# One-hots of an edge-block builder, made with one vector instruction per tile and a key per partition in place of one instruction per eight tiles

## The reference, cut to what matters

```python
def _L0_gnn_ref(x, edge_index, edge_weight, fc_w, fc_b, conv_w, conv_b, bn_gamma, bn_beta):
    ...
    h = relu(_bn(x @ fc_w + fc_b, bn_gamma[0], bn_beta[0]))
    for i in range(2):
        z = _aggregate(h, row, col, edge_weight) @ conv_w[i] + conv_b[i]   # segment_sum(val * h[row], col)
        z = relu(_bn(z, bn_gamma[i + 1], bn_beta[i + 1]))
        h = z + h
    return h
...
def _fa_layer(h, row, col, Wt_l, bt_l, Wg_l, bg_l):      # layer L3, twice
    h = h @ Wt_l.T + bt_l
    deg = clip(segment_sum(ones(row.shape), row, n), 1.0)
    dinv = deg ** (-0.5)
    g = tanh(h[row] @ Wg_l + bg_l)
    norm = g * dinv[row] * dinv[col]
    return segment_sum(norm[:, None] * h[row], col, n) + h
```

## Time and profile before

| | |
|---|---|
| median of the runs | 3548.09 us (3545.02 to 3555.73, 3 runs) |
| the profiled execution's own time | 3552.29 us |
| its span (first to last instruction) | 3550.4 us |
| mean granted TensorE clock | 0.714 of full speed |
| busy over the span: PE, PEld, DVE, ACT, POOL | 2215.2, 1972.0, 2218.8, 1284.5, 2026.6 us |
| L2063, one-hots of the packs | 264 instructions, 171.0 us, 691 ns each |
| pass 1: first gather, last gather | 1180.49 us, 1726.44 us after the span's start |

### The profile page before, as it was taken

One profiled execution on the slowest core, in us unless ns is written; L12 is line 12 of the kernel. 1 busy time (PEld: TensorE's weight loads), 2 busy tenths in 40 slices (PEclk: granted clock), 3 DMA queues, 4 the chain that ended last, 5 costly groups with the idle time before them and its releaser, 6 DMA issues.

```text
span 3550.4 us, 56998 instructions
## 1 busy us (share of the span) xinstructions
PE 2215.2 (62%) x15272; PEld 1972.0 (56%) x15273; DVE 2218.8 (62%) x5812; ACT 1284.5 (36%) x3489; POOL 2026.6 (57%) x2076
## 2 busy tenths in 40 slices
PE   4991240566665556766556756735555555999998
PEld 3991230455554345555456656725444453998998
DVE  8997961777776645555536656575787777433434
ACT  4220020233222123333356777735777774000000
POOL 1777777777776577777357777716777770000000
PEclk9995555666666665565565565567778777999999
DMA  2210000111213222333333333325444441221222
GB/s 84 69 57 4 4 22 28 49 53 53 52 53 44 57 71 87 89 88 89 49 93 78 80 80 77 71 15 155 132 131 128 130 117 25 73 75 52 68 74 63
DMA packets 171613, 249.97 MB, mean 70 GB/s; under 512 B 52006, under 2 KB 120412, under 8 KB 171154
## 3 DMA queue, kind: packets, MB, share of 16 engines
q0 software_dynamic: 72704, 138.94, 16.7%
q1 hardware_dynamic: 94276, 96.20, 9.4%
q10 hardware_dynamic: 4430, 12.43, 1.1%
HBM read 217.00 MB, written 30.41 MB: 70 GB/s over the span
## 4 chain that ended last, share of the span: by engine, by line
POOL 47%; PE 22%; issue 17%; DVE 8%; ACT 3%; DMA 2%; DVEq 1%; POOLq 0%; ACTq 0%; SPq 0%
POOL arena L715 20%; POOL pool L715 17%; PE psum L1505 8%; POOL rec_dram L692 7%; PE psum L1501 5%; POOL ACC L715 2%; PE psum L1231 2%; PE psum L1425 2%; DVE ACC L2339 1%; ACT pool L888 1%; PE psum L1269 1%; ACT pool L816 1%; DMA arena<-tab_dram,tblk 1%; PE psum L1106 1%; DVE pool L1726 1%
## 5 line engine op out<-in xcount | busy, mean ns | idle before, releaser
L715 POOL DMA_INDIRECT arena<-tab_dram,tblk x832 | 797.5, 959 | 411.0 <-issue 250.3
L692 POOL DMA_INDIRECT rec_dram<-arena,ACC x400 | 396.3, 991 | 195.9 <-issue 119.1
L715 POOL DMA_INDIRECT pool<-tab_dram,arena x416 | 402.6, 968 | 131.9 <-issue 126.5
L1552 PE MATMUL psum<-pool 128*128 128x136 f32 (+1 forms) x1664 | 362.0, 399 | 81.0 <-DVE pool L2263 74.8
L1552 PEld LDWEIGHTS psum<-pool 128*128 128x128 f32 x1664 | 335.6, 290 | 92.7 <-issue 51.3
L1383 PE MATMUL psum<-pool 128*128 128x128 f32 x832 | 193.1, 426 | 301.1 <-DMA pool<-tab_dram,arena 228.1
L2119 DVE CAST pool<-pool 128x1024 f32<-128x1024 uint8 x264 | 182.3, 694 | 278.4 <-PE psum L1505 168.2
L1383 PEld LDWEIGHTS psum<-pool 128*128 128x128 f32 x832 | 180.0, 328 | 305.5 <-DVE pool L2132 134.6
L715 POOL DMA_INDIRECT pool<-tab_dram,tblk x272 | 276.2, 1015 | 125.9 <-issue 79.9
L857 ACT ACTIVATE arena<-psum,key 128x128 bf16<-128x128 f32 x416 | 146.4, 377 | 479.1 <-PE psum L1326 479.1
L1505 PE MATMUL psum<-arena,pool 128*128 128x128 f32 x2504 | 300.2, 277 | 0.0
(11 more groups left out here) (373 smaller groups left out, 4923.8 us busy)
## 6 DMA issues: line engine op xcount, KB each, us to landing
pool<-items_dram SPq DMA_DIRECT2D x264, 128.0 KB, 2.0
pool<-dst_dram SPq DMA_DIRECT2D x104, 256.0 KB, 3.5
items_dram<-pool SPq DMA_DIRECT2D x132, 128.0 KB, 1.7
arena<-tab_dram,tblk POOLq DMA_INDIRECT x832
HN<-in_edge_attr_dram ACTq DMA_DIRECT2D x23, 500.0 KB
pool<-tab_dram,arena POOLq DMA_INDIRECT x416
rec_dram<-arena,ACC POOLq DMA_INDIRECT x400, 2.1
pool<-tab_dram,tblk POOLq DMA_INDIRECT x272
```

Of the source, the lines that this page charges most:

```text
L692: nc.gpsimd.indirect_dma_start(rec_dram, bass.IndirectOffsetOnAxis(ap=row_all[:, c:c + 1], axis=0), rec_all[:, c, :], None).then_inc(s_sca ...
L715: nc.gpsimd.indirect_dma_start(to[:, j, :], None, tab_dram[k], bass.IndirectOffsetOnAxis(ap=idx[:, G * g + j:G * g + j + 1], axis=0)).then ...
L1552: last_ = nc.tensor.matmul(bank[j // 3][:, (j % 3) * ww:(j % 3 + 1) * ww], OHF[:, half, j, :], weighed[k][:, half, j, :], start=True, stop ...
```

## The change

The key tables become float32 with one entry per key (as many bytes as before, since every key stood there twice in bf16). ACT's and DVE's writes into them lose the doubling. Where one instruction made a side's one-hot for eight items, eight instructions make it, one per item; each compares the same row `iotab` of 128 bf16 numbers with one key per partition, which it takes as a scalar operand from the float32 table. The last of the eight on each side signals. The numbers that come out are the same.

```diff
-        ends = [MT[:, 1216 + ITEMS * i:1216 + ITEMS * (i + 1)].bitcast(BF16).rearrange("p (w a) -> p w a", a=2) for i in range(2)]
+        ends = [MT[:, 1216 + ITEMS * i:1216 + ITEMS * (i + 1)] for i in range(2)]
...
-                        nc.scalar.activation(ends[e][:, lo:hi, :], bank[7][:, 0:hi - lo].unsqueeze(2).to_broadcast([P, hi - lo, 2]),
-                                             ACT.Copy).then_inc(s_itemc, 1)
+                        nc.scalar.activation(ends[e][:, lo:hi], bank[7][:, 0:hi - lo], ACT.Copy).then_inc(s_itemc, 1)
...
-                link(v.tensor_tensor(ends[0][:, FIRSTS:ITEMS, :], recS[:, :, R_SRC].unsqueeze(2).to_broadcast([P, TILES, 2]),
-                                     later_behind[:, :].unsqueeze(2).to_broadcast([P, TILES, 2]), ALU.add))
-                link(v.tensor_copy(ends[1][:, FIRSTS:ITEMS, :], recS[:, :, R_DST].unsqueeze(2).to_broadcast([P, TILES, 2])))
+                link(v.tensor_tensor(ends[0][:, FIRSTS:ITEMS], recS[:, :, R_SRC], later_behind[:, :], ALU.add))
+                link(v.tensor_copy(ends[1][:, FIRSTS:ITEMS], recS[:, :, R_DST]))
...
                 for e in range(2):
-                    v.tensor_tensor(onehots[slot][e].rearrange("p (w n a) -> p w n a", w=PACK, a=2),
-                                    iotab.rearrange("p (n a) -> p n a", a=2).unsqueeze(1).to_broadcast([P, PACK, P // 2, 2]),
-                                    ends[e][:, bass.ds(PACK * b, PACK), :].unsqueeze(2).to_broadcast([P, PACK, P // 2, 2]),
-                                    ALU.is_equal).then_inc(s_itemv, 1)
+                    for j in range(PACK):
+                        last_ = v.tensor_scalar(onehots[slot][e][:, P * j:P * (j + 1)], iotab, ends[e][:, bass.ds(PACK * b + j, 1)], None, ALU.is_equal)
+                    last_.then_inc(s_itemv, 1)
```

## The result

The changed kernel took 3530.69 us (median of 4 runs, 3526.88 to 3533.53), the kernel before 3547.64 us beside it (4 runs, 3545.02 to 3555.73). The ratio is 0.9939, 95% interval 0.9925 to 0.9953: 17 us by the medians, 22 (17 to 27) by the ratio. The forecast was a gain of 14, to 3534. The profiled execution took 3526.88 us, its span is 3525.0.

The account below looks back on a forecast made before the run. POOL's gathers were taken to bound the end of pass 1, with PE and ACT nearly equal. Gathers 15 us shorter, less about 1 for waits, make 14: from the median 3548.1 to 3534 us, range 3526 to 3590.

Parts of the forecast that it names:

- POOL's path decides: In pass 1 POOL never waits for a ring slot, and the end of the pass waits for its gathers.
- 346 x 0.043 = 15 us: Saving on POOL in pass 1: 346 gathers going from a mean of 1.003 to 0.960 us.
- less about 1: Taken off the 15 us for waits between DVE, PE and POOL, nearly equal in pass 1's loop, leaving 14.
- That 10.25 us is PE's floor.: In pass 1 PE with ACT needs 10.25 us a group even where its rows are there in time.
- DVE's terms: New one-hots on DVE in pass 1: 0.163 us per instruction start to start, 9.9 us of work a group.
- The bounds 0.034 us apart for the two element rates: One new DVE instruction: 0.196 to 0.204 us at the plain element rate, 34 ns less if bf16 doubles it.
- The break-even of 0.174: Above 0.174 us per new one-hot instruction DVE becomes the bound; each further ns costs 2.1 us.
- The stalls at the jump back: DVE stands 4.57 us for its instructions at the loop's jump back, 13.4 us together in the pass.
- the row that spoke for the plain rate: A single one-source bf16 to bf16 DVE instruction, 0.46 us for 416 elements, with a gather running beside it.
- Gathers that don't get faster (2): Rival: POOL's gather mean stays near 1.00 us, or DVE lags a little; 3539 to 3556 us, chance 0.24.
- POOL locked out (4): Rival: each gather waits out half a 0.25 us vector instruction, mean 1.07 us; 3571 us, chance 0.08.
- Case 3: Rival: DVE becomes the bound, over 0.174 us per instruction; 0 to +19 us or 3594 to 3611 us, chance 0.22.

Follow-up runs that it names:

- none3: The changed kernel with the one-hots of the first three packs only, used again by the other 129 packs: 3529.53 us, ratio 0.9929 to the kernel before.
- onemore4: The changed kernel with one more tensor_scalar a pack, 80 elements into a spare place: 3543.69 us, ratio 0.9969 to the kernel before.
- longts: The changed kernel with one tensor_scalar of 128x1024 per side and pack, one key for all eight items: 3538.87 us, ratio 0.9956 to the kernel before.

## Why the prediction was right or wrong

**Right: POOL's path decides.** The last gather moved by 19.3 us in the pass and PE's end followed. With nearly no one-hots to make (none3) the pass is 1.8 us shorter and no more.

**The step that failed: the term "346 x 0.043 = 15 us", with its "less about 1".** The sum had 14 us for POOL's path and the runs showed 19.3. Two parts of the term were too small. The gathers went to 0.956, not 0.960: 1.4 us. And the window of that term began at 1275 us, one row after the gather of 3.80 us, which only the kernel before had: 2.85 us. It stood beside the six one-hots that the earlier trace rows shows; I had read their row and not POOL's beside it. "Less about 1 for waits between three nearly equal engines" found nothing to pay for. 14 + 1.4 + 2.85 + 1 = 19. The ratio makes the gain 22 us with an interval from 17; what it has above 19 no row places, and the part of the span behind the pass scatters by 8 us.

**Wrong: "That 10.25 us is PE's floor."** The groups at 10.26 and 10.22 us of the earlier trace rows had POOL's pace, not PE's own. POOL's timeline of the kernel before in the same stretch, two gathers that are eight apart:

```profile
1488.20 1.03 POOL L715 DMA_INDIRECT ACC<-tab_dram,tblk  x1 [0.30 <-PE psum L1454]
...
1498.43 1.04 POOL L715 DMA_INDIRECT ACC<-tab_dram,tblk  x1 [0.30 <-PE psum L1454]
```

They start 10.23 us apart. PE's own rows are 8.2 us of the group (1489.89 to 1498.12), at a granted clock of 0.50 (1.2 GHz); the 2.0 us ahead of each group's first product were a wait for what the next group needs, not a fixed cost. In the changed kernel group 13 starts 8.22 us after group 12 (1316.57 to 1324.79), at the same clock of 0.50. The 6.83 us of the kernel without one-hots were measured at a clock of 1.00, so they bound PE's floor only at that clock. With the floor as put, PE would have started group 49 at 1699; it did at 1688.21. That the forecast survived is luck: POOL needs 10.05 us a group itself, and so the wrong floor changed the sum little.

**Right: DVE's terms.** One instruction was put at 0.163 us: undisturbed it is (7.91 - 0.24) / 47 = 0.163, with gathers beside it 0.168. The group was put at 9.9: it is 9.85 where DVE runs alone (from 2392.25 to 2402.10), 10.1 with gathers. The bounds 0.034 us apart for the two element rates: 0.033. The break-even of 0.174 was put too high: it takes the end of the kernel before (1741) and not one that POOL's gain has moved. The changed kernel had 8.7 us to spare, 0.004 us an instruction, which makes it 0.168 + 0.004 = 0.172; onemore4, with some 20 us more work and a pass 11.7 us longer, shows it. So DVE did not set the end, but it was nearer than the prediction had it, and in groups 40 to 47 it was the bound. The stalls at the jump back were put at 13.4 us and were 4.1. Why the row that spoke for the plain rate, was so long was not tried; the gather beside it may have done it.

**The rivals.** Gathers that don't get faster (2) and POOL locked out (4) did not come. But the mechanism of 4 is real. The Trainium skill (SBUF — State Buffer, "Who interferes with whom") has a one-source instruction in a two-port mode lock GpSimd out until it ends; longts shows it, gathers slowed to 0.975 us by a tensor_scalar of 0.5 us. By its other half a tensor_tensor with two SBUF inputs collides only with GpSimd's reads, and that descriptor writing is left alone is called inferred there. The rows show that it holds gathers: instructions of 0.69 and 1.22 us did so until they ended. But an indirect gather also reads its row numbers from SBUF (`tblk` in its rows), so this need not be against the rule; no run here tells whether the read or the writing of descriptors is what waits. The price in the prediction, half an instruction for each gather, was too high since the first 0.12 us of waiting are free. Case 3 holds on the slow chips, by another way than the one given: an instruction takes no longer there (0.163 us from start to start), but DVE stands 127 us between them, for nothing that the profile shows.

## What to carry to other kernels

Where POOL issues gathers back to back and sets the end of a stage, look for DVE instructions of over 0.2 us with all data in SBUF beside it: what they cost grows faster than their length (0.057 us a gather at 0.69 us, 0.216 at 1.22). Short one-source instructions, or pieces with a wait between them, give it back; short two-input instructions in an unbroken run make it worse. The price is in instructions: eight for one was worth 0.6% on one kind of chip and cost 1.7% on another, so a change of this kind is to be timed on more than one.

## What was not expected of the hardware

- Engines do not wait for each other only at semaphores, as was said ahead of the prediction. Here POOL waits for DVE without one: a held gather ends 0.82 us after the DVE instruction; with nothing in the way it lasts 0.94 us. A DVE instruction with an input in PSUM (1.21 us long) holds nobody, and neither does one that began less than 0.05 us before the gather.
- An unbroken run of two-input instructions holds one gather throughout: 3.80, 4.49, 6.63 and 7.02 us.
- Chips differ: the same kernel took 3548 to 3556 us on three sets of runs, and 4685 to 4709 us on three others, on the latter with long waits that no row explains.
- The stall of DVE at the loop's jump back fell from 4.57 to 1.50 us though the loop's code had grown threefold.
